# Two VectorE-sized jobs taken from GpSimd, and a new order of work, in a fused scan and mixture-of-experts kernel

## What is computed

```python
def combine(c1, c2):
    a1, b1 = c1; a2, b2 = c2
    return (a2 * a1, a2 * b1 + b2)
# attention part: xn = layernorm(x)
g = sigmoid(einsum('bld,ed->ble', xn, Wg) + bg)
h = associative_scan(combine, (1 - g, g * xn), axis=1)      # a recurrence along the sequence
x = x + layernorm(einsum('bld,ed->ble', h, Wo) + bo)
# expert part: xf = layernorm(x), N tokens, E = 8 experts, C = 320 places each
eid = argmax(softmax(xf @ router_w + router_b))
rank = number of earlier tokens with the same expert; valid = rank < C
y_tok = relu(buf @ w1 + b1) @ w2 + b2     # for tokens that have a place in their expert's buffer
yov = relu(xf @ ow1 + ob1) @ ow2 + ob2    # for all other tokens
x = x + layernorm(y_tok or yov)
```

## Time and profile before

| what | us |
|---|---|
| median of 3 runs | 1272.75 (1271.8 to 1273.87) |
| the profiled execution | 1271.02 |
| its span, from first to last instruction | 1269.3 |
| TensorE busy in the span | 1172.6 |
| VectorE busy | 1003.3 |
| ScalarE busy | 772.5 |
| GpSimd busy | 810.3 |

### The profile page before, as it was taken

The page is one execution under the profiler, slowest core; times in us unless marked ns, Lnnn a source line. Parts: engine busy times, 40 slices in busy tenths (PEclk is TensorE's granted clock), DMA queues, the critical chain, the costliest instruction groups (busy, mean ns, idle before and its releaser), DMA issues. The chain is left out here.

```text
span 1269.3 us, 24820 instructions
## 1 busy us (share of the span) xinstructions
PE 1172.6 (92%) x7705; PEld 1038.1 (82%) x7705; DVE 1003.3 (79%) x2731; ACT 772.5 (61%) x1362; POOL 810.3 (64%) x887
## 2 busy tenths in 40 slices
PE   4499999999999999999999999999999999889994
PEld 4388888888888888888888888888888888789994
DVE  4688888888888888888888888888888876578882
ACT  4265666666666666666666666666665655477773
POOL 4456666666666666666666666666666664436774
PEclk9699999999999999999999999999999999999997
DMA  7211111111111110100111110011111100334430
GB/s 242 83 35 50 51 47 44 38 37 34 33 33 33 33 33 33 33 26 24 33 33 33 33 33 25 25 33 33 33 33 33 33 17 18 104 112 168 149 103 31
DMA packets 59688, 65.32 MB, mean 51 GB/s; under 512 B 7836, under 2 KB 55886, under 8 KB 59525
## 3 DMA queue, kind: packets, MB, share of 16 engines
q1 hardware_dynamic: 52484, 59.58, 14.5%
q0 software_dynamic: 7168, 5.32, 1.4%
HBM read 40.17 MB, written 38.87 MB: 62 GB/s over the span
## 5 line engine op out<-in xcount | busy, mean ns | idle before, releaser
L362 POOL TENSOR_TENSOR rstd<-veps,mhalf 128x4 f32<-128x4 f32 (+1 forms) x144 | 179.4, 1246 | 355.1 <-DVE nmean L712 355.1
L539 ACT ACTIVATE hid<-psH,biasT 128x512 f32<-128x512 f32 (+1 forms) x320 | 209.1, 653 | 264.4 <-PE psH L1010 259.2
L1108 PE MATMUL psY<-W_hi,hid_hi 128*128 128x256 f32 x1216 | 351.2, 289 | 0.9 <-DVE hid_lo L833 0.9
L1111 PE MATMUL psY<-W_hi,hid_lo 128*128 128x256 f32 x1216 | 344.2, 283 | 0.0
L1110 PE MATMUL psY<-W_lo,hid_hi 128*128 128x256 f32 x1216 | 344.0, 283 | 0.0
L833 DVE TENSOR_TENSOR hid_lo<-hid,hid_hi 128x512 fp32r<-128x512 f32 (+1 forms) x320 | 266.0, 835 | 89.3 <-ACT hid_hi L543 83.8
L1008 PE MATMUL psH<-xfT_hi,W_hi 128*128 128x512 f32 (+1 forms) x640 | 246.1, 385 | 5.5 <-DVE xfT_lo L777 2.9
L1010 PE MATMUL psH<-xfT_hi,W_lo 128*128 128x512 f32 (+1 forms) x640 | 242.5, 379 | 0.0
L1009 PE MATMUL psH<-xfT_lo,W_hi 128*128 128x512 f32 (+1 forms) x640 | 242.3, 379 | 0.0
L1108 PEld LDWEIGHTS psY<-W_hi,hid_hi 128*128 128x128 f32 x1216 | 230.2, 189 | 10.5 <-DVE hid_lo L833 1.8
L1110 PEld LDWEIGHTS psY<-W_lo,hid_hi 128*128 128x128 f32 x1216 | 230.0, 189 | 6.7
(11 more groups left out here) (110 smaller groups left out, 2186.6 us busy)
## 6 DMA issues: line engine op xcount, KB each, us to landing
xin<-L_attn_x SPq DMA_DIRECT2D x32, 512.0 KB, 3.5
stage<-L_ffn_w SPq DMA_DIRECT2D x16, 1024.0 KB, 6.2
out<-outt SPq DMA_DIRECT2D x32, 512.0 KB, 2.9
xbuf<-zrow SPq DMA_DIRECT2D x1, 2570.0 KB, 18.5
xin<-xbuf SPq DMA_DIRECT2D x8, 257.0 KB, 5.5
stage<-L_ffn_ow SPq DMA_DIRECT2D x2, 1024.0 KB, 10.3
xbuf<-x,idx POOLq DMA_INDIRECT x128
b_b<-L_ffn_b SPq DMA_DIRECT2D x1, 1024.0 KB, 13.5
```

Source lines behind the costliest of these rows:

```text
L362: pool.tensor_tensor(rstd[k][:, 0:n], veps[k][:, 0:n], mhalf[:, 0:n], ALU.pow).then_inc(s_rs[k], 1)
L539: act.activation(hid[j % 2][:, 0:n], psH[:, j % 2, 0:n], ACT.Relu, bias=bias).then_inc(s_hid, 1)
L1108: pe.matmul(psY_t[:, t, :], hi, w[0][:, j, :], start=(j == 0 and t % 2 == 0), stop=False, skip_group_check=True)
L1111: last = pe.matmul(psY_t[:, t, :], lo_, w[0][:, j, :], start=False, stop=(j == HC - 1), skip_group_check=True)
```

## The change

Seven edits. (1) `state_lo` goes from GpSimd's stream, where it was last in a step, to VectorE's, between `result(now)` and `stats3(now)`. (2) `residual2` goes from GpSimd's stream, behind `norm0`, to VectorE's, behind `stats1(nxt)`; for the last group it stands behind `lo` 4 of the first expert. (3) `stats1(nxt)` follows `attended(nxt)` at once, ahead of `lo` 2. (4) `place(now)` moves ahead of `lo` 3, and `rank(now)` on TensorE from j = 4 to j = 3. (5) On VectorE `residual1` moves to directly behind `lo` 3, and the reads of `stats2` go ahead of `xn_lo(far)`, its aggregates behind it; `lo` 4 and 5 follow together. (6) On ScalarE `norm1(nxt)` goes ahead of `xn_hi(far)` and `relu` 4. (7) In the start, the two `state_lo` are on VectorE as well.

```diff
@@ GpSimd, step and its helpers
                 if live(far, NG):
                     norm0(far)
-                if live(prev, NG):
-                    residual2(prev)
                 if live(nxt, NG):
                     deviation(1, nxt, TG)
...
                 if live(now, NG):
                     dispatch(now, range(TG))
-                if live(far, NG):
-                    state_lo(far)
...
             norm0((0, 1))
-            state_lo((0, 0))
             deviation(1, (0, 0), TG)
             norm2((0, 0), x1, TG)
-            state_lo((0, 1))
...
             norm2((0, 1), xe, ET, NG)
-            residual2(last_group)
             keep_rows((0, 1))
@@ ScalarE, step
                 hidden(range(2, 4))
+                if up:
+                    norm1(nxt)
                 if ahead:
                     xn_hi(far)
                 hidden(range(4, 5))
-                if up:
-                    norm1(nxt)
@@ VectorE
+            def state_lo(g):
+                i, v = g
+                dve.wait_ge(s_wo, cnt(g, 2, 0))
+                for c in range(DC):
+                    dve.wait_ge(s_h_hi, cnt(g, 2, c + 1))
+                    dve.tensor_tensor(hst_lo[:, c, :], hst[v][:, c, :], hst_hi[:, c, :].bitcast(F32), ALU.subtract)\
+                        .then_inc(s_h_lo, 1)
...
+            def residual2(g):
+                i, v = g
+                dve.wait_ge(s_z, cnt(g, 1, 1))
+                if live(grp(i, v, -2), NG):
+                    dve.wait_ge(s_st_out[v], landed(grp(i, v, -2)))
+                dve.tensor_tensor(outt[v][:], ysb[:], x1[v][:, :, 0:D], ALU.add).then_inc(s_out, 1)
...
                 if up:
                     attended(nxt)
+                    stats1(nxt)
+                if live(grp(i, u, -1), NG):
+                    residual2(grp(i, u, -1))
                 low(2)
+                if run:
+                    place(now)
+                low(3)
                 if up:
-                    stats1(nxt)
-                low(3)
+                    residual1(nxt)
+                    read_rows2a(nxt)
                 if ahead:
                     xn_lo(far)
-                if run:
-                    place(now)
-                low(4)
                 if up:
-                    residual1(nxt)
-                    stats2(nxt)
-                low(5)
+                    moments(2, nxt, TG)
+                low(4, 5)
...
+                if ahead:
+                    state_lo(far)
                 if run:
                     stats3(now, TG)
...
+                    if j == 4 and not live(prev, E):
+                        residual2((NG // 2 - 1, 1))
@@ TensorE, step
-                        if j == 4:
+                        if j == 3:
                             rank(now)
```

More of the change, by code:

```diff
@@ L405, in norm2 @@
                 last.then_inc(s_tok2, 1)
[L407 to L413, removed]
             def step(i, u):
@@ L768, in residual1, with read_rows2a @@
                 dve.tensor_tensor(x1[v][:, :, 0:D], att[:], xin[v][:], ALU.add).then_inc(s_x1, 1)
+            def residual2(g):
[4 more added lines that the diff above has]
+                dve.tensor_tensor(outt[v][:], ysb[:], x1[v][:, :, 0:D], ALU.add).then_inc(s_out, 1)
+            def read_rows2a(g):
+                dve.wait_ge(s_x1, cnt(g, 1, 1))
+                read_rows(2, lambda t: x1[g[1]][:, t, 0:D], TG)
             def stats2(g):
-                dve.wait_ge(s_x1, cnt(g, 1, 1))
-                stats(2, lambda t: x1[g[1]][:, t, 0:D], g, TG)
+                read_rows2a(g)
+                moments(2, g, TG)
             def xf_lo(g, n, base=0):
@@ L937, in _ @@
             recurrence((0, 0))
+            state_lo((0, 0))
             dve.wait_ge(s_rw_hi, 1)
@@ L949, in _ @@
             xf_lo((0, 0), GT)
+            state_lo((0, 1))
             stats0((1, 0))
```

## The result

| | us | against the kernel before beside it |
|---|---|---|
| changed kernel, the recorded runs (4) | 1283.47 (1282.21 to 1287.53) | before 1272.28; ratio 1.0092, 95% interval 1.0067 to 1.0116 |
| the same program, c1_changed (4) | 1236.91 (1234.28 to 1240.04) | before 1270.07; 0.9738, 0.9721 to 0.9754 |
| the same program, c3_changed (4) | 1238.36 (1237.11 to 1239.34) | before 1271.69; 0.9739, 0.9718 to 0.9761 |
| the same program, c4_changed (2) | 1239.52 (1236.71 to 1242.32) | before 1272.33; 0.9741, 0.9709 to 0.9772 |

The recorded result is slower by 0.9% where I had forecast faster by 3%, so the forecast is wrong. But the same program, run again three times, each time on another chip, was faster by 2.6%, 5 to 8 us above my 1232 (on which chip the recorded runs were made is not known).

The account below looks back on a forecast made before the run. TensorE's work plus T1's waits for `tok2` (54.2 us) was taken as the bound. Savings of 28.8 + 0.8 + 3.4 + 1.6 + 4.2 = 38.8 us from 1271.0 gave 1232; 1224 to 1240 had 0.61, the range reaching 1250.

Parts of the forecast that it names:

- The steady step: Each of 30 steps loses T1's wait of 1.16 us and gains 0.20 at the gate: 28.8 us saved.
- step (a): Steady step, `residual1` to `xn_lo` on VectorE: done at 436.35, gate uncovered and waiting 0.2 us (bounds 0 and 0.7).
- Step (b): Steady step, `norm2` on GpSimd: ends between 442.9 and 443.5, T1's wait of 1.16 us gone with 1.4 to spare.
- starvation rival: `norm2` gets held up beside the recurrence and `lo` 6; T1 waits 0.45 us a step, 1246 us, chance 0.14.
- The rule: VectorE instructions with two SBUF inputs and GpSimd instructions reading SBUF block each other fully; with it the sum would be 25.
- The edges: The start, the last two steps and the change of experts: 10.0 us saved together, 5.0 at the lower bounds.
- Steps 29 and 30: An ordinary step's gain, then 3.4 us (2 to 4.4) in step 30 from a shorter chain to T1 and regained clock.
- Step 31: `dispatch`, the first expert's load and T1 hang on `place`, now needing `lo` 2 alone: 1.6 us earlier (1 to 1.6).
- From expert 0 to 1: The last residual, on VectorE, ends 3.3 us sooner and the next weights leave sooner: 4.2 us saved (2 to 5).
- the errors of my walk between `stats3` and `xn_lo`: Rival: the uncovered gate becomes each step's wait, at the bound 0.7 us; 1247 us, or 1252 with low edges; chance 0.2.
- "slower" rival: Moved jobs cost GpSimd's 2.56 and 2.39 us on VectorE; gate waits 1.8 a step (deciding from 1.5), 1280 us, chance 0.04.

Follow-up runs that it names:

- c2_before: The kernel before, run again untouched for its trace: 1272.09 us (one execution).
- e9: The kernel before, with `result` on VectorE also waiting for the signal of the next step's first block of layer 1: 1267.66 us, ratio 0.9978.
- e8: The changed kernel, with `result` on VectorE also waiting for the signal of the next step's first block of layer 1: 1295.21 us, ratio 1.0195.
- e5: The changed kernel with `state_lo` back on GpSimd behind the scatters, the last residual left on VectorE: 1228.81 us, ratio 0.9681.
- e7: The changed kernel with `state_lo` back on GpSimd and the four scatters issued ahead of `norm2`: 1228.21 us, ratio 0.9665.
- e10: The changed kernel with `state_lo` back on GpSimd and `result` held back to 1.6 us behind the step's start: 1247.39 us, ratio 0.9798.
- the first four experiments: Changed kernel with scatters ahead of `norm2` (1239.24 us), plain DMAs (1239.26), last scatter behind layer 2 (1246.10), or both moved jobs on GpSimd (1240.59).
- the control: The changed kernel run again, untouched: 1236.91 us, ratio 0.9738.

## Why the forecast was wrong, and what of it was right

**The steady step, with signals on time: right.** From the start of the step (416.72 where I walked it, 342.07 in c1_changed), forecast and measured: reads of `stats1` 8.9 and 8.8; power 11.3 and 11.1, drawn out to 1.91 and 1.93; `norm1` 13.6 and 13.4; `residual1` 15.8 and 15.6; `xn_lo` done 19.6 and 19.4. Timeline of VectorE in that step of c1_changed, beside the earlier trace rows:

```profile
350.83 1.41 DVE L678 BATCH_NORM_STATS2 st<-att 128x6 f32<-128x256 f32 x4
...
353.05 1.23 DVE L761 TENSOR_TENSOR outt<-ysb,x 128x1024 f32<-128x1024 f32 x1
...
357.66 1.23 DVE L754 TENSOR_TENSOR x<-att,xin 128x1024 f32<-128x1024 f32 x1 [0.93 <-ACT att L527]
...
360.24 1.28 DVE L711 TENSOR_TENSOR xnT_lo<-xnT,xnT_hi 128x512 fp32r<-128x512 f32 x2
...
361.44 0.37 DVE L685 BATCH_NORM_AGGREGATE mv<-st 128x2 f32<-128x6 f32 x4
```

and of GpSimd and ScalarE, beside the earlier trace rows:

```profile
353.21 1.93 POOL L362 TENSOR_TENSOR rstd<-veps,mhalf 128x4 f32<-128x4 f32 x1 [0.78 <-DVE nmean L690]
...
364.17 5.64 POOL L403 TENSOR_SCALAR tok<-x,rstd,nmr 128x256 f32<-128x256 f32 x4 [0.24 <-POOL nmr L364]
...
369.98 1.11 POOL L383 DMA_INDIRECT xbuf<-x,idx  x1 [0.17 <-issue]
...
355.45 1.09 ACT L527 ACTIVATE att<-att,nmr,rstd 128x256 f32<-128x256 f32 x2 [0.55 <-POOL nmr L364]
```

The instruction behind `xn_lo` starts at 361.44 and the gate at 361.62. The cover is used up to within 0.2 us, as my step (a) had it.

**The gate's wait: right in size, wrong in shape.** I took 0.2 us in 30 steps, 6.0 in all; c1_changed waits 7.9, as 0.6 in every second step and nothing in the others:

```profile
314.82 1.29 DVE L830 TENSOR_TENSOR hid_lo<-hid,hid_hi 128x512 fp32r<-128x512 f32 x2 [0.33 <-issue]
...
346.86 0.69 DVE L830 TENSOR_TENSOR hid_lo<-hid,hid_hi 128x512 fp32r<-128x512 f32 x1
...
329.80 0.47 PE L1013 MATMUL psA<-xnT_hi,WgT_hi 128*128 128x512 f32 x1 [0.60 <-issue]
```

The steps differ ahead of `lo` 0: VectorE reaches it 4.79 us behind the start of a step, and 5.23 where its loop turns, with 0.33 of idleness that no work explains. I had walked only the step without it.

**Step (b), `norm2`: right that it does not wait, wrong on its length.** I left 3.79 us for it. It took 5.64 beside the recurrence and ended 0.33 ahead of T1, where I had 1.4 to spare. That is the starvation rival, to within 0.4 us of coming true. The rule that I had set beside it, of the Trainium skill's "SBUF — State Buffer", "Who interferes with whom", points the right way, but c1_changed shows no wait of T1 in the loop, and blocking in part only: beside the residual, which took 1.23, the power took 1.93 and not 1.41.

**The edges.** Steps 29 and 30 give 4.3 us (c2_before 33.3 and 32.6, c1_changed 31.8 and 29.8); I had 0.96 + 3.4. Step 31 as forecast: T1 ahead of expert 0 waits 2.77 and not 4.46, 1.7 us for my 1.6. From expert 0 to 1 I had 4.2 and little came. Timelines of TensorE, GpSimd and VectorE in c1_changed:

```profile
1073.00 1.54 PE L1069 MATMUL psT<-ident,tok 128*128 128x128 f32 x6 [2.77 <-POOL tok L403]
...
1092.07 1.03 PE L1069 MATMUL psT<-ident,tok 128*128 128x128 f32 x6 [2.22 <-POOL tok L403]
...
1086.69 2.43 POOL L403 TENSOR_SCALAR tok<-xin,rstd,nmr 128x256 f32<-128x256 f32 x1 [0.24 <-POOL nmr L364]
...
1087.04 1.22 DVE L761 TENSOR_TENSOR outt<-ysb,x 128x1024 f32<-128x1024 f32 x1
```

The residual ends 12.5 us behind the start of expert 0 where it ended 16.7 behind in c2_before, and the next weights leave 4.2 earlier, more than my 3.3. Their wait is gone (3.17 in c2_before), but the second expert's T1 now waits 2.22 for a normalization whose first instruction takes 2.43 beside that residual. This term, which I mis-sized, is one of three for which 1237 was measured and not 1232. Between the spans of c2_before and c1_changed lie 32.0 us, where my sum has 38.8:

| | forecast | measured |
|---|---|---|
| up to the start of step 1 | 1.8 | 3.6 |
| steps 1 to 28 | 26.9 | 21.9 |
| steps 29 and 30 | 4.4 | 4.3 |
| step 31 | 1.6 | 1.6 |
| experts | 4.2 | 0.6 |

(Against the trace I walked, the first row is 2.3.) The 28 steps fell short because the wait of T1 was worth 1.08 us (32.91 a step in c2_before against the 31.83 of a step of c1_changed without a wait), not 1.16, and the gate's wait 0.3 on average, not 0.2.

**What failed.** The term that failed is the gate's wait in step (a): 0.2 us, at most 0.7, where the recorded run has 1.3 to 2.0 in 22 steps, 37.7 us in all, and a lower clock behind six of them. It fell at a step which I did not write down as one: I started every walk with `result` 0.2 us behind the start of the step, and there it came 1.74 to 1.95 behind. The trace in front of me had 0.8 in every second step. There it was free, and the kernel before hides even 1.4 (e9). The change spends just this slack: it takes the gate's cover from 2.9 us to 0.1, so that each microsecond of a late `result` is one of TensorE: in e8, where it is 1.4 late, a step with 0.6 at the gate has 2.0 and one with none has 1.3. I did price the errors of my walk between `stats3` and `xn_lo`, up to 0.7 a step, but not one that comes in at its top. My "slower" rival had the right point (a gate wait of 1.5 us a step) and nearly the right time, 1280, with the wrong cause; the jobs cost 1.23 and 1.28 (a pair) on VectorE, not GpSimd's prices. Its 0.04 was too little for a wait that any delay upstream can make.

**What stays open.** Shown is that a late `result` costs what was lost, and that in the recorded traces completion signals near scatters were late. Why they were there is not shown. The five chips of the later runs had none, with the same program and the scatters at the same moments, so H could not be tested: no experiment met a late signal. All four recorded executions took the long time, so whether that belongs to a chip or to an occasion isn't told apart either. That the scatters cause them is argued from two traces only, from where the late signals stand and from their fixed distance to the scatter in one. Nor does any run tell whether the recording of the trace has a part in it; both traces with late signals lack records too. Whether e5 or e7 would hold its gain on the recorded chip was not seen; e10 stands in for it.

## What to carry to other kernels

Before an order is made tighter, note for each wait that the change uncovers how much slack it leaves, and what each microsecond of delay at the top of the chain then costs; holding one signal back by hand (e8, e9) tells in one run whether a version survives it. Read two neighbouring steps and not one: both the late `result` and the turn of VectorE's loop stood in every second step. Where a result contradicts a walk that matches the trace otherwise, run the unchanged program again before looking for causes in it: three of the first four experiments came out as the theory of the late signals had it, and the control took that away.

## What the runs showed of the hardware

One program, 1283 us in its recorded runs and 1237 to 1240 in three later ones, with the kernel before at 1270 to 1272 everywhere. In the recorded traces a completion signal of TensorE came up to 1.76 us late if a scatter had been issued within the last 4 us, and never more than 0.01 late otherwise (333 and 367 signals). The Trainium skill, in "DMA: Bandwidth & Descriptors", "Why a DMA increments its semaphore by 16 and not by 1", says that a DMA from GpSimd's queue signals from all 16 engines; c1_changed agrees, with 2048 landings recorded on the scatters' two semaphores (128 x 16), and the recorded run shows 884. That the missing ones have the same cause as the late ones is a guess. A wait of 1.92 us at the gate was followed by a granted clock of 0.63 in the next 4.6 us; the clock fell behind six of the 13 waits of 1.9 to 2.0, and waits of 0.6 left it at 1.00 in c1_changed. Where its loop turned, VectorE idled for 0.33 us there, which showed only because the gate had no cover left.
